# The last third of a four-layer kernel in one block: RWKV mixing with weights padded to the full array, norms, output, feed-forward and store by chunks

## What is computed

```python
x = norm(x + attention(x))        # 16 heads of 64, full softmax, rotary
x = norm(x + local_layers(x))     # 2 x (windowed attention + GEGLU feed-forward)
x = norm(x + rwkv(x))             # below
x = norm(x + (silu(x @ wg.T) * (x @ wu.T)) @ wd.T)    # hidden 384, int weights / 127

# rwkv
delta = shifted(x) - x
low = tanh((x + delta * mu_x) @ W_x1)                 # 5 x 32 columns
mus = einsum('blnr,dnr->blnd', low, W_x2) + x_bias    # five mixes
xr, xw, xk, xv, xg = [x + delta * mus[:, :, i] for i in range(5)]
r, k, v = xr @ W_r, xk @ W_k, xv @ W_v
w = -exp(tanh(xw @ W_w1) @ W_w2 + b_w2); g = xg @ W_g
# scan over time, 16 heads: o_t = r_t (S + u k_t v_t); S = exp(w_t) S + k_t v_t
o = groupnorm(o) * gn_w + gn_b                        # groups of 8 values
rwkv = (o * g * sigmoid(g)) @ W_o
```

## Time and profile before

| | us |
|---|---|
| runs shown | 1987.57, 1983.98, 1982.47 (median 1983.98) |
| the profiled execution's own time | 1981.65 |
| its span, first to last instruction | 1979.9 |
| busy: PE / DVE / ACT / POOL | 1782.2 / 1439.9 / 1437.3 / 1409.4 |
| end of the local layers in the span | 1736.6 |
| mixing, from its first product to the first of the scan | 1746.1 to 1804.85 |
| scan | 1804.85 to 1885.0 |
| group norm and output | 1885.3 to 1913.8 |
| feed-forward | 1922.0 to 1965.1 |
| issue of the store | 1973.36 |

### The profile page before, as it was taken

The page is one execution under the profiler, slowest core; times in us unless marked ns, Lnnn a source line. Parts: engine busy times, 40 slices in busy tenths (PEclk is TensorE's granted clock), DMA queues, the critical chain, the costliest instruction groups (busy, mean ns, idle before and its releaser), DMA issues. The chain is left out here.

```text
span 1979.9 us, 54360 instructions
## 1 busy us (share of the span) xinstructions
PE 1782.2 (90%) x23072; PEld 1109.6 (56%) x23072; DVE 1439.9 (73%) x2638; ACT 1437.3 (73%) x1755; POOL 1409.4 (71%) x797
## 2 busy tenths in 40 slices
PE   5999999999999999999999999768999999769936
PEld 1466666666666666666666666664565666333523
DVE  5787877877878778787787776148978888344764
ACT  1688888888888888888888899427988888422421
POOL 3699899899899899899899899756655666022000
PEclk8899999999999999999999999888999999768968
DMA  4101101011011010110100100411111111000000
GB/s 115 29 18 29 25 22 29 21 26 29 18 29 25 22 29 21 26 29 21 26 23 24 26 10 2 134 42 43 43 37 35 40 35 32 5 1 0 0 0 22
DMA packets 71018, 56.59 MB, mean 29 GB/s; under 512 B 29164, under 2 KB 64312, under 8 KB 70776
## 3 DMA queue, kind: packets, MB, share of 16 engines
...
## 5 line engine op out<-in xcount | busy, mean ns | idle before, releaser
L304 POOL TENSOR_TENSOR ah_probs_lo<-ah_probs,ah_probs_hi 128x1024 f16<-128x1024 f32 x512 | 1081.1, 2133 | 130.8 <-ACT ah_probs L496 130.7
L553 DVE TENSOR_REDUCE ah_part_max<-ah_p_m 128x1 f32<-128x512 f32 x1024 | 682.7, 686 | 185.4 <-PE ah_p_m L368 170.2
L493 ACT ACTIVATE ah_probs_hi<-ah_p_s 128x1024 f16<-128x1024 f32 x512 | 524.2, 1024 | 181.7 <-PE ah_p_s L387 161.1
L496 ACT ACTIVATE ah_probs<-ah_p_s 128x1024 f32<-128x1024 f32 x512 | 521.1, 1018 | 0.0
L401 PE MATMUL ah_p_o<-ah_v_hi,ah_probs_hi 128*128 128x65 f16 x4096 | 477.0, 195 | 34.3 <-DVE a_attn L568 28.9
L405 PE MATMUL ah_p_o<-ah_v_hi,ah_probs_lo 128*128 128x65 f16 x4096 | 476.5, 194 | 0.0
L403 PE MATMUL ah_p_o<-ah_v_lo,ah_probs_hi 128*128 128x64 f16 x4096 | 476.4, 193 | 0.0
L401 PEld LDWEIGHTS ah_p_o<-ah_v_hi,ah_probs_hi 128*128 128x128 f16 x4096 | 383.3, 98 | 140.8 <-DVE a_attn L568 59.8
L403 PEld LDWEIGHTS ah_p_o<-ah_v_lo,ah_probs_hi 128*128 128x128 f16 x4096 | 378.8, 98 | 96.8
L368 PE MATMUL ah_p_m<-ah_k_hi_lo,ah_q_hi_twice 128*128 128x512 f16 x1024 | 393.4, 385 | 7.1 <-DVE ah_part_max L553 5.6
L386 PE MATMUL ah_p_s<-ah_q_hi_twice,ah_k_hi_lo 128*128 128x512 f16 x1024 | 388.8, 380 | 0.3 <-ACT ah_probs L496 0.3
...
## 6 DMA issues: line engine op xcount, KB each, us to landing
...
ah_q_hi_twice<-ah_hi SPq DMA_DIRECT2D x128, 64.0 KB, 2.0
...
```

What stands on the lines that cost most here:

```text
L304: pool.tensor_tensor(pl[:, p % RW, :, :], pb[:, p % RP, :, :], ph[:, p % RW, :, :], ALU.subtract).then_inc(lo_pool, 1)
L493: act.activation(ph[:, p % RW, :, :], p_s[:, p % 2, :, :], ACT.Exp, scale=HD ** -0.5)
L496: act.activation(pb[:, p % RP, :, :], p_s[:, p % 2, :, :], ACT.Exp, scale=HD ** -0.5).then_inc(exp_done, 1)
L553: dve.tensor_reduce(part[:, t, 2 * half + b:2 * half + b + 1], p_m[:, b, :], AX, ALU.max).then_inc(maxed, 1)
```

## The change

Blocks 1 to 8 above become one function with one block, `phase_tail` (prefix `t_`). Everything before, up to the end of `local_layers`, stays.

- Weights: `wx1` is padded from 160 to 256 columns, `W_x2` becomes five 128x128 blocks with zeros outside their 32 rows, `ww1` is padded to 128 columns and `ww2` to 128 rows. The gate product is one product with `wg` as the weights, so that the gate lies with features on partitions.
- The three layer norms go by chunk: statistics on DVE, the root on POOL as a power of -0.5 in four small operations, all 16 normalisations on ACT.
- Group norm, turning, scaling and output of chunk c-1 and c-2 stand between the steps of the scan of chunk c. The group norm's weight and bias are applied on ACT after the turn, the gate on POOL. The root of the group norm is a square root on ACT, once per chunk.
- The feed-forward starts on chunk 0 as soon as the scan has ended, with the rest of the output in its gaps. Its weights are loaded at the start of the block and converted in the first two steps of the scan. Each chunk is stored when it is normalised (4 DMAs of 256 KB).
- The scan's state is kept for all chunks, without the copy of its last column.

```diff
-                phase_local(nc, x_sb, ident, ln, local)
-            phase_rwkv(nc, x_sb, ident, a, ln, late)
-            phase_int_ffn(nc, x_sb, ident, a, ln, late)
-        store_block(nc, x_sb, out)
+                local_layers(nc, x_sb, ident, local)
+                clear_semaphores(nc)
+            phase_tail(nc, x_sb, ident, a, late, out)
...
+    wide = lambda w: c(np.pad(w, ((0, P - w.shape[0]), (0, -w.shape[1] % P))))
+    a["wx1"] = wide(i["L1_attn_W_x1"])
+    wx2 = np.zeros((P, MIXES, D), f)
+    for k, block in enumerate(i["L1_attn_W_x2"].transpose(1, 2, 0)):
+        wx2[LR * (k % 4):LR * (k % 4 + 1), k] = block
+    a["wx2"] = wx2
...
+                def mixes(c):
+                    pe.wait_ge(low_done, 2 * c + 2)
...
+                        low = low_a if i < MIXES - 1 else low_b
+                        pe.matmul(p_kr[:, n % 2, :], wx2[:, i, :], low[:, c % 2, :], start=True,
+                                  stop=True).then_inc(mu_ready, 1)
...
+                turn_x(0)
+                turn_x(1)
+                pe.wait_ge(late.mix_in, late.MIX)
+                first(0)
+                turn_x(2)
+                for c in range(NCH):
+                    mixes(c)
+                    if c + 1 < NCH:
+                        first(c + 1)
+                    decay_gate(c)
+                    if c == 0:
+                        turn_x(3)
...
+                    if h == 3 and c >= 1:
+                        turn_o(c - 1)
+                    if h == 1 and c >= 2:
+                        out_y(c - 2)
...
+                turn_x2(0)
+                gate_up(0, 0)
+                out_y(CLAST - 1)
+                gate_up(0, 1)
+                turn_x2(1)
+                gate_up(0, 2)
+                gate_up(1, 0)
+                turn_o(CLAST)
+                down(0)
+                gate_up(1, 1)
...
+                norm(0, 0)
+                copy_x(0)
+                norm(0, 1)
+                copy_x(1)
+                low(0)
+                norm(0, 2)
+                copy_x(2)
+                low(1)
+                decay_gate(0)
+                norm(0, 3)
+                copy_x(3)
...
+                    if h == 0 and c == CLAST:
+                        norm(1, 0)
+                    if h == 1 and c >= 1:
+                        square(c - 1)
+                    if h == 2 and c >= 1:
+                        root(c - 1)
+                    if h == 3 and 1 <= c < CLAST:
+                        scale_o(c - 1)
...
+                def ln_root(k, c):
+                    b, ts = 3 * c, tiles(c)
+                    pool.wait_ge(var_done[k], TPC * (c + 1))
+                    pool.tensor_scalar(veps[:, k, ts], mv[:, k, ts, 1], LN_EPS, None, ALU.add).then_inc(root_step[k], 1)
+                    pool.tensor_scalar(nmean[:, k, ts], mv[:, k, ts, 0], -1.0, None, ALU.mult).then_inc(root_step[k], 1)
+                    pool.wait_ge(root_step[k], b + 2)
+                    pool.tensor_tensor(lrstd[:, k, ts], veps[:, k, ts], neg_half[:, :], ALU.pow).then_inc(root_step[k], 1)
+                    pool.wait_ge(root_step[k], b + 3)
+                    pool.tensor_tensor(shift[:, k, ts], nmean[:, k, ts], lrstd[:, k, ts],
+                                       ALU.mult).then_inc(shift_done[k], 1)
...
+                    if h == 1 and c >= 1:
+                        centre(c - 1)
+                    if h == 2 and c >= 1:
+                        sum_squares(c - 1)
+                        if c >= 2:
+                            residual(c - 2)
+                    if h == 3 and c >= 1:
+                        invert(c - 1)
+                        if c >= 2:
+                            dve.wait_ge(res_done, c - 1)
+                            ln_stats(1, c - 2)
```

More of the change, by code:

```diff
@@ new lines, in phase_tail @@
+        bn_done = [sc.sem(f"bn_done{k}") for k in range(3)]
+        var_done = [sc.sem(f"var_done{k}") for k in range(3)]
+        root_step = [sc.sem(f"root_step{k}") for k in range(3)]
+        shift_done = [sc.sem(f"shift_done{k}") for k in range(3)]
+        normed = [sc.sem(f"normed{k}") for k in range(3)]
+        CONSTS = 2
+        heads = lambda t: t.rearrange("p (g v) -> p g v", v=V_C)
+        each = lambda t: t.rearrange("p (t d) -> p t d", d=D)
+        tok = lambda c: slice(c * CH, (c + 1) * CH)
@@ L1652, in out @@
                     if h == 0 and c >= 2:
-                        pe.wait_ge(o_done, c - 1)
+                        pe.wait_ge(oc_done, c - 1)
                     for t in range(TPC):
@@ new lines, in down @@
+                def down(c):
+                    pe.wait_ge(hidden, HC * (c + 1))
+                    if c >= 2:
+                        pe.wait_ge(fin_done, c - 1)
+                    else:
+                        pe.wait_ge(oc_done, CLAST + c)
+                    for t in range(TPC):
+                        for k in range(HC):
+                            mm = pe.matmul(p_o[:, c % 2, t * P:(t + 1) * P], hT[:, c % 2, k, t * P:(t + 1) * P],
+                                           wf[:, 2, k * P:(k + 1) * P], start=(k == 0), stop=(k == HC - 1))
+                    mm.then_inc(d_ready, 1)
@@ new lines, in _ @@
+                turn_x(0)
[3 more added lines that the diff above has]
+                turn_x(2)
+                for c in range(NCH):
+                    mixes(c)
[4 more added lines that the diff above has]
+                        turn_x(3)
+                pe.wait_ge(late.scan_in, late.SCAN)
+                pe.wait_ge(late.out_in, late.OUT)
@@ L1678, in _, with norm @@
+                gate_up(1, 1)
+                out_y(CLAST)
+                gate_up(1, 2)
+                turn_x2(2)
+                gate_up(2, 0)
+                down(1)
+                gate_up(2, 1)
+                gate_up(2, 2)
+                turn_x2(CLAST)
+                gate_up(3, 0)
+                down(2)
+                gate_up(3, 1)
+                gate_up(3, 2)
+                down(CLAST)
             @block.scalar
             def _(act):
+                def norm(k, c):
+                    act.wait_ge(shift_done[k], c + 1)
+                    for t in range(c * TPC, (c + 1) * TPC):
+                        act.activation(x_sb[:, t, :], x_sb[:, t, :], ACT.Identity, scale=lrstd[:, k, t:t + 1],
+                                       bias=shift[:, k, t:t + 1]).then_inc(normed[k], 1)
@@ new lines, in _ @@
+                    if h == 1 and c >= 1:
[4 more added lines that the diff above has]
+                        scale_o(c - 1)
+                norm(1, 1)
+                scale_o(CLAST - 1)
+                copy_x2(0)
+                square(CLAST)
+                tanh_f(0, 0)
+                root(CLAST)
+                tanh_f(0, 1)
+                copy_x2(1)
+                tanh_f(0, 2)
@@ new lines, in _ @@
+                tanh_f(1, 0)
+                norm(1, 2)
+                scale_o(CLAST)
+                tanh_f(1, 1)
+                tanh_f(1, 2)
+                copy_x2(2)
+                tanh_f(2, 0)
+                norm(1, CLAST)
+                tanh_f(2, 1)
+                tanh_f(2, 2)
+                copy_x2(CLAST)
+                norm(2, 0)
+                tanh_f(3, 0)
+                tanh_f(3, 1)
+                norm(2, 1)
+                tanh_f(3, 2)
+                norm(2, 2)
@@ L1704, in _ @@
+                delta_z(1)
+                for c in range(NCH):
+                    for i in range(MIXES):
+                        part(c, i)
+                        if i == 2 and c >= 1:
+                            gate_g(c - 1)
+                    if c == 0:
+                        ln_stats(0, CLAST)
+                    if c + 2 < NCH:
+                        delta_z(c + 2)
+                gate_g(CLAST)
                 dve.wait_ge(late.scan_in, late.SCAN)
-                dve.memset(st[:, :, 0, 0:1], 0.0).then_inc(zeroed, 1)
```

760 lines of the change are left out of this document (394 added, 366 removed).

## The result

The changed kernel takes 1925.44 us (median of 4 runs, 1923.93 to 1926.03), the kernel before 1983.22 (4 runs beside them). The ratio is 0.9709, 95% interval 0.9696 to 0.9721. The gain is 57.8 us where 47 was forecast, and the time lies 4.6 us under the forecast's range. The profiled execution took 1925.85, with a span of 1924.0.

A forecast was written before the change was run, and what follows sets the result against it. PE was taken to bound mixing, scan and feed-forward. Starting the scan 11.5 us earlier, -6.6 in it and 42.2 behind it saved 47.1 of 1979.9: span 1932.8, forecast median 1937 us, range 1930 to 1951.

The forecast's parts named there:

- A: From the start of the tail (first norm's statistics) to the first mix product: 15.6 us.
- C: Mixing of chunks 1 to 3, assuming a full clock when PE is supplied without gaps: 26.6 us.
- D: From the end of the mixing to the scan's first kv, with w, exp, v, k and a table load: 4.4 us.
- F: From the last kv to the last instruction, with feed-forward, last norm and store: 58.1 us.
- E: The scan, first to last kv: 15 steps as before 68.9, inserted turns and outputs 4.6, two stalls: 75.5 us.
- the two stalls of 1 us: In the scan, two places where an inserted PE product waits, 1 us each.
- Rival 1: In the scan, DVE's and PE's additions add up: 16.1 us more instead of 6.6, total 1946.5; chance 0.17.
- B: Mixing of chunk 0, with PE starting cold, up to the turn of chunk 3: 14.7 us.
- The step to the median: Added to the profiled execution's forecast of 1934.5 us: 2.33, giving 1936.9.
- Rival 2: The clock alternates in the mixing as before, half the chunks slow: 11 us more, 1948; chance 0.15.
- Rival 3: The clock is slow in all of the mixing: 28 us more, 1965; chance 0.06.
- the scan at half clock: Padding and short waits keep PE slow into the scan: 8.5 us a step against 4.64, up to 2026; chance 0.03.

The follow-up runs named there:

- experiment 1: The changed kernel with the scan's decay product (w) contracted over its true 64 rows again instead of 128: 1931.04 us.
- experiment 2: The kernel before with only the scan's product for w padded to 128 rows: 1978.31 us against 1982.21, ratio 0.998.
- experiment 3: The changed kernel with the five mix products of a chunk contracted over their true 32 rows: 1936.91 us.
- experiment 4: The kernel before, order unchanged, with mixing products and w padded as in the change and feed-forward weights loaded earlier: 1967.73 us against 1982.21, ratio 0.9925.
- experiment 5: The changed kernel with the scan's w, v, k, r and sum over keys all contracted over 64 rows, leaving out terms: 1989.96 us, ratio to before 1.0037.

## Why the prediction was wrong

**A, C, D and F, 104.7 us of forecast, were right within 0.9 us together, in part by luck.** In A, POOL's root with its power took 1.94 a chunk at the start, where I had 1.4 (the power alone 1.04), and z's second product gave that back, 1.22 instead of 1.84. In C the second chunk took 9.72 with its slow mixes, the third 8.39, the fourth 8.40, where I had 9.1, 9.1 and 8.4. In F the first gate product stood 7.4 behind the last kv instead of 5.1, and PE's work from there on was 36.2 instead of 38.7, mainly because a turn takes 0.44 at full clock, and I had 4.8 for five. The table loads fell into ACT's idle, and the store took 3.6 where I had 4.0.

**E failed.** Its first term was "15 steps as before, 68.9". The change list says that ww2 gets 128 rows, and I priced that at nothing without saying so. The measured step is 4.33, which is -4.0 over 15 steps; experiments 1 and 2 show that the one product's width is the whole reason. The trace of the kernel before had it, in lines that I didn't read: from k on, products stand 0.86 and 0.85 apart (1818.26, 1819.12, 1819.97), but it is 0.91 from the sum over keys to w, 1.05 from w to v and 0.97 from v to k. Five gaps of 0.86 would make 4.3, and the step was 4.64. A bound engine that is 0.3 slower than that, with no wait named, has an item that I didn't price. The range could not catch it either: its cheap bounds touch the store, the power and the stalls, and the first term of E had no bound. (They add up to 1932, so the 1930 of the range has no sum behind it.) With this term right the forecast would have been 1933, still 7.5 too long.

The second term was mis-sized. "Three times four turns, 0.9 each" took the turn from the earlier trace rows, which had run at the low clock; at full clock it is 0.47. The third turn also lies behind the last kv. Two turns and two outputs are 2.5 instead of 4.6 (2.9, less the 0.09 that comes back behind each). Third, the two stalls of 1 us never came. -4.0, -2.1 and -2.0 are 8.1; 0.4 to 0.5 of it was lost again at the start of the scan, where PE waited 1.07 for pr (at 1801.88) and the first three k took 9.10 in place of 8.66. That leaves the 7.6. Rival 1 (DVE's additions add up) fell too: DVE has no idle in the steps with inserts, but falls behind only once, at the end, where PE waits 2.16 for the last pr.

**The mixing was right in its sum and wrong in its reason.** I wrote that "with PE supplied without gaps the clock is full", and that padding costs nothing because POOL's add takes longer. Experiments 3 to 5 say otherwise: in the order of before the clock is 0.97 with 128 rows and 0.70 with 32, in the new order 0.87 and 0.67, and without any gap and with 64 rows in the scan 0.51. The padding isn't free here, it is the gain: 12 us in the mixing of the changed kernel. Where I weighed what the Trainium skill says of narrow products against the change, both sides of the scale held the wrong thing: side-by-side products saved PE time that it didn't lack.

Two rows were also misread, without weight in the sum. The 1.84 between z's products is from start to start, and the 1.02 of r is a duration. From start to start r takes 0.85 (1819.12 to 1819.97 in the earlier trace rows), so the two levels are 2.2 apart and not 1.8. And DVE has one wait in a scan step, of 1.14 or 1.06, not both.

**B** was 1.9 too long, mainly because the clock was full before the third mix began (0.50 up to 1757.0, 1.00 from 1757.8), so that four mixes took 5.3 where I had 6.7.

**The step to the median** was wrong by 2.7. I added the 2.33 by which three runs of before stood above their profiled one. Those three spread over 5 us, and the runs of the changed kernel stand at theirs.

**The rivals.** None of them was the way it went. Rival 2, the alternating clock, came true in small, in the second chunk's mixes: 1.5 where it had 11. Its reason against was that these chunks wait for nothing but POOL; the turn's wait of 2.58 for ACT stood right ahead of these mixes. Rival 3's 28 is 26 by its own terms. The one on the other side, the scan at half clock, came true in experiment 5, where I brought it about: 8.54 a step for the 8.5 that the prediction worked out, and slower than before. Its condition was wrong: it named short waits and padding, and in that run it was narrow products.
